# The softplus of a Mamba block summed by TensorE in an open PSUM bank

## The reference

```python
dt = jax.nn.softplus(dt_low @ W_dt + b_dt)      # 512 tokens x 512 channels
h = exp(dt_t[..., None] * A) * h + (dt_t * x_t)[..., None] * B_t[:, None, :]
y = einsum('bds,bs->bd', h, C_t)
y = (y + x * D) * silu(z);  return y @ W_out
```

## Time and profile before

| | |
|---|---|
| three executions | 4346.42, 4347.93, 4351.42 us, median 4347.93 |
| the profiled execution | 4355.29 us, its span 4353.5 us |
| busy share of TensorE, VectorE, ScalarE, GpSimd | 90%, 89%, 54%, 40% |
| granted TensorE clock, mean | 0.968 of 2.4 GHz |

### The profile page before, as it was taken

One profiled execution on the slowest core, in us unless ns is written; L12 is line 12 of the kernel. 1 busy time (PEld: TensorE's weight loads), 2 busy tenths in 40 slices (PEclk: granted clock), 3 DMA queues, 4 the chain that ended last, 5 costly groups with the idle time before them and its releaser, 6 DMA issues.

```text
span 4353.5 us, 55576 instructions
## 1 busy us (share of the span) xinstructions
PE 3935.7 (90%) x18933; PEld 2043.7 (47%) x18933; DVE 3872.0 (89%) x5708; ACT 2366.9 (54%) x4341; POOL 1724.7 (40%) x1295
## 2 busy tenths in 40 slices
PE   5878889999999999999999999998989999998898
PEld 3333444444545445454544545454444545544555
DVE  7699989898998989899898989989899899998753
ACT  2444455656555565555556465565545656564544
POOL 1254434443434435353343444444344344433410
PEclk9989999999999999899999999999899999999999
DMA  2699787878778787876787777788786888878511
GB/s 64 160 209 219 173 210 167 203 161 191 181 166 202 177 202 166 185 192 160 184 188 188 178 178 189 164 209 174 167 199 140 207 171 218 177 183 190 135 55 42
DMA packets 241440, 753.50 MB, mean 173 GB/s; under 512 B 37650, under 2 KB 132659, under 8 KB 171524
## 3 DMA queue, kind: packets, MB, share of 16 engines
q1 hardware_dynamic: 241156, 749.95, 73.7%
HBM read 647.30 MB, written 101.71 MB: 172 GB/s over the span
## 4 chain that ended last, share of the span: by engine, by line
DVE 40%; PE 33%; DMA 10%; issue 9%; ACT 6%; POOL 1%; SPq 1%; DVEq 0%; ACTq 0%; POOLq 0%
DVE state L1767 11%; DVE mt L1846 6%; DVE u L1762 4%; PE m L1249 4%; DMA state<-dtx_scratch 3%; PE m L1276 3%; PE pd L1477 2%; DMA decay<-dt_scratch 2%; PE y L1350 2%; DMA gz_scratch<-front 2%; DVE front L1701 2%; PE y L1338 2%; DVE front L1672 2%; DVE front L1676 2%; DVE front L1578 1%
## 5 line engine op out<-in xcount | busy, mean ns | idle before, releaser
L824 POOL TENSOR_TENSOR state<-state,bc 128x1024 f32<-128x1024 f32 x512 | 1270.4, 2482 | 1305.8 <-DVE u L1762 1287.1
L1767 DVE TENSOR_TENSOR_SCAN state<-decay,u 128x1024 f32<-128x1024 f32 x512 | 1166.8, 2279 | 6.4 <-ACT decay L1050 1.7
L1050 ACT ACTIVATE decay<-decay,a_neg 128x511 f32<-128x511 f32 x1024 | 674.9, 713 | 168.3 <-DMA decay<-dt_scratch 167.6
L1249 PE MATMUL m<-w_gu,hats_m 128*128 128x480 f32 x1472 | 680.5, 582 | 67.1 <-DVE front L1676 44.5
L1762 DVE TENSOR_TENSOR u<-state,bc 128x1024 f32<-128x1024 f32 x512 | 640.8, 1252 | 45.1 <-DMA state<-dtx_scratch 36.4
L1249 PEld LDWEIGHTS m<-w_gu,hats_m 128*128 128x128 f32 x1472 | 255.4, 192 | 334.5 <-issue 154.6
L805 POOL TENSOR_TENSOR front<-front,hsc_m 128x704 f32<-128x704 f32 x128 | 199.3, 1557 | 509.3 <-DVE front L1581 509.3
L1276 PE MATMUL m<-w_dn,front 128*128 128x256 f32 x1476 | 366.4, 390 | 14.1 <-ACT front L983 13.2
L1196 PE MATMUL y<-minus,zero 128*128 128x512 bf16 x1292 | 341.8, 389 | 2.1 <-ACT vec L904 2.1
L1338 PE MATMUL y<-state,sel 128*32 128x512 f32 x2048 | 280.6, 621 | 47.6 <-POOL state L824 47.3
L1276 PEld LDWEIGHTS m<-w_dn,front 128*128 128x128 f32 x1476 | 270.1, 191 | 103.8 <-ACT front L983 48.8
(11 more groups left out here) (396 smaller groups left out, 7278.3 us busy)
## 6 DMA issues: line engine op xcount, KB each, us to landing
decay<-dt_scratch SPq DMA_DIRECT2D x256, 1024.0 KB, 7.4
state<-dtx_scratch SPq DMA_DIRECT2D x256, 1024.0 KB, 11.5
qk_scratch_main<-shared SPq DMA_DIRECT2D x60, 384.0 KB, 4.3
shared<-qk_scratch_main SPq DMA_DIRECT2D x360, 64.0 KB
kh<-qk_scratch_main SPq DMA_DIRECT2D x360, 64.0 KB
xs_scratch<-front SPq DMA_DIRECT2D x16, 1024.0 KB, 9.5
dt_scratch<-front SPq DMA_DIRECT2D x256, 64.0 KB, 2.7
dtx_scratch<-hats_m SPq DMA_DIRECT2D x256, 64.0 KB, 5.0
```

The costliest lines, as they stand in the source:

```text
L824: eng.tensor_tensor(st, st, bc[:, 1:2, :].to_broadcast([P, WIDE, L]), ALU.mult).then_inc(scan_pool.sem, scan_pool.step(f"c{r}{h}"))
L1050: ins = eng.activation(d, d, ACT.Exp, scale=a_neg[:, g:g + 1])
L1249: mm = eng.matmul(f.bank(r, f"gu{t}{p}")[:, 0:2 * width], norm.hat_t[:, k, t * P:(t + 1) * P], w_gu[:, k, 2 * lo:2 * (lo + width)], start= ...
L1767: eng.tensor_tensor_scan(st, decay[:, n % ND, h * WIDE * L:(h + 1) * WIDE * L], u[:, :], 0.0, ALU.mult, ALU.add).then_inc(scan_dve.sem, sc ...
```

## The change

The logits are halved: `w_dt`, with the bias in its last row, is multiplied by 0.5 once at the start. Since max(a, 0) = a/2 + |a/2|, the whole softplus becomes a sum of six terms in the open bank: a/2, |a/2|, -(1 + ex) rounded, 1, ex and ln(1 + ex). TensorE adds each of the last five as an fp32 product with the identity (the constant 1 as a product of one row of ones with one row of ones). VectorE loses `rest`, `log` and `dt`, and reads the bank for `dtx`. ScalarE copies the sum out into `dt`, tokens 1 to 511. Two banks are used as before, in pairs of chunks.

```diff
 PE, head:
+    for first in (0, 2):
+        pair = (first, first + 1)
+        for c in pair:
+            # waits: c >= 2: ACT "dt{c - 2}"
+            matmul(MB[(1+c)%2], w_dt[:, c*P:(c+1)*P], pj, start=True, stop=False)    # dt{c}
+        for c in pair:
+            # waits: ACT "abs{c}"
+            matmul(MB[(1+c)%2], ident, lnx[:, c%2, :])                               # half{c}
+        for c in pair:
+            # waits: ACT "one{c}"
+            matmul(MB[(1+c)%2], ident, dt[:, c%2, :])
+            matmul(MB[(1+c)%2], ones[0:1].to_broadcast([1, P]), ones[0:1].to_broadcast([1, L]))
+            matmul(MB[(1+c)%2], ident, ex[:, c%2, :])                                # rest{c}
+        for c in pair:
+            # waits: ACT "ln{c}"
+            matmul(MB[(1+c)%2], ident, lnx[:, c%2, :], stop=True)                    # log{c}
-    matmul(MB[(1 + c) % 2], w_dt[...], pj, start=True, stop=True)   # waits: DVE "dt{c-2}"
 ACT:
+    mul(w_dt[:, :], w_dt[:, :], 0.5)                                # once, at the start
 ACT, head:
-    activation(ex, MB, Abs);  activation(ex, ex, Exp, scale=-1.0);  activation(dt, ex, Identity, bias=ones)
+    activation(lnx, MB, Abs); activation(ex, lnx, Exp, scale=-2.0)
+    activation(dt, ex, Identity, bias=less_one, scale=-1.0)
     activation(lnx[:, b, :], ex[:, b, :], Ln, bias=1.0)             # now after PE "half"
+    activation(dt[:, b, 1:L], MB[(c + b) % 2][:, 1:L], Copy)        # waits: DVE "dtx"
 DVE, head:
-    scalar_tensor_tensor(dt, dt, -1.0, ex, add, subtract)           # rest
-    tensor_tensor(lnx, lnx, dt, subtract)                           # log
-    scalar_tensor_tensor(dt, MB, 0.0, lnx, max, add)                # dt
-    tensor_tensor(dtx, dt, xs, mult)
+    tensor_tensor(dtx, MB[(1 + c) % 2], xs[:, c, :], mult)          # waits: PE "log{c}"
     memset(dt[:, b, 0:1], 0.0)
```

More of the change, by code:

```diff
@@ L96 @@
[L96 to L98 removed]
+        "11110000000000000000101201110001122111112222222222222222212122222222222211112221112222222222222122122112222222222222211222222111"
@@ L297, in build @@
         eps = sb("eps", [P, T])
-        ones = sb("ones", [P, 1])
+        ones, less_one = sb("ones", [P, 1]), sb("less_one", [P, 1])
         xx = sb("xx", [P, NX, T, D])
@@ L500, in build @@
         CONVS = [("conv", 0)] + [e for m in range(1, C) for e in (("conv", m), ("tanh", m - 1))] + [("tanh", C - 1)]
-        head_pe = Steps(sem("head_pe"), ["x0", "x1"] + [f"in{m}" for m in range(C)] + ["pj"] + [f"dt{c}" for c in range(C)]
+        head_pe = Steps(sem("head_pe"), ["x0", "x1"] + [f"in{m}" for m in range(C)] + ["pj"] + [f"{n}{c}" for b in (0, 2) for n in ("dt", "half", "rest", "log") for c in (b, b + 1)]
                         + [f"in{C + m}" for m in range(C)])
         head_act = Steps(sem("head_act"), ["x0", "x1"] + [f"{n}{m}" for n, m in CONVS] + ["pj"]
-                         + [f"{n}{c}" for b in (0, 2) for part in (("abs", "exp", "one"), ("ln",)) for c in (b, b + 1) for n in part] + [f"tanhz{m}" for m in range(C)])
+                         + [f"{n}{c}" for b in (0, 2) for part in (("abs", "exp", "one"), ("ln",), ("dt",)) for c in (b, b + 1) for n in part] + [f"tanhz{m}" for m in range(C)])
         head_dve = Steps(sem("head_dve"), [n for w, m in CONVS for n in ((f"tap{m}1", f"tap{m}2", f"tap{m}3") if w == "conv" else (f"silu{m}",))]
-                         + [f"{n}{c}" for c in range(C) for n in ("rest", "log", "dt", "dtx", "zero")] + [f"siluz{m}" for m in range(C)])
+                         + [f"{n}{c}" for c in range(C) for n in ("dtx", "zero")] + [f"siluz{m}" for m in range(C)])
         scan_pe = Steps(sem("scan_pe"), [n for r in range(ROUNDS) for n in ([f"skip{r // Q}"] if r % Q == 0 else []) + [f"sum{r}"]] + [f"o{t}" for t in range(T)])
@@ L772, in _ @@
             eng.memset(ones[:, :], 1.0)
+            eng.memset(less_one[:, :], -1.0)
             eng.memset(w_dn[:, IK - 1, :], 0.0)
@@ L1023, in head @@
                         eng.wait_ge(dt_saved[c % 2], 64 * (2 * i + 1))
-                    eng.activation(dt[:, c % 2, :], ex[:, c % 2, :], ACT.Identity, bias=ones[:, :]).then_inc(head_act.sem, head_act.step(f"one{c}"))
+                    eng.activation(dt[:, c % 2, :], ex[:, c % 2, :], ACT.Identity, bias=less_one[:, :], scale=-1.0
+                                   ).then_inc(head_act.sem, head_act.step(f"one{c}"))
                     if c % 2:
-                        yield
-                        if c >= 2:
-                            eng.wait_ge(head_dve.sem, head_dve.after(i, f"dt{c - 2}"))
                         for b in range(2):
+                            yield
+                            eng.wait_ge(head_pe.sem, head_pe.after(i, f"half{c - 1 + b}"))
                             eng.activation(lnx[:, b, :], ex[:, b, :], ACT.Ln, bias=1.0
                                            ).then_inc(head_act.sem, head_act.step(f"ln{c - 1 + b}"))
+                        for b in range(2):
+                            yield
+                            eng.wait_ge(head_dve.sem, head_dve.after(i, f"dtx{c - 1 + b}"))
+                            eng.activation(dt[:, b, 1:L], MB[(c + b) % 2][:, 1:L], ACT.Copy).then_inc(head_act.sem, head_act.step(f"dt{c - 1 + b}"))
                 for m in range(C):
```

352 lines of the change are left out of this document (181 added, 171 removed).

## The result

The changed kernel takes 4543.46 us, median of three executions (4536.49 to 4562.05), against 4347.93. The ratio is 1.0463, with a 95% interval of 1.0432 to 1.0495. The profiled execution took 4543.46 us, its span is 4541.7 us, which is 188 us more than before, and the granted clock has a mean of 0.982 (0.968 before).

What follows compares the result with a forecast made beforehand. TensorE's queue, late in the dt stretch, was taken to bound the kernel there: +215 for products, +13 for new waits, -56 for the clock make +172 us on 4355.3, less 7 to the median: 4520 us, range 4410 to 4630.

Steps and rivals of the forecast that it cites:

- products, seq. 3 to 15: Dt stretches of thirteen sequences: added fp32 products lengthen TensorE's work by 18.8 us a sequence, 244 us.
- keepers: TensorE's filler products in the dt stretches of sequences 3 to 15: nearly all of 19.5 us go, 16 us taken off.
- idle time filled: TensorE's idle 23.4 us in the dt stretches of sequences 3 to 15 is filled by added products, 23 us off.
- clock: Dt stretches: most drops to a lower TensorE clock go, giving back 56 us; bounds -110 and +66.
- sequences 0 to 2: Pipeline fill: 56 us added against 54 us of slack, mostly in the first two; 10 us for the third.
- new waits: dt2 waits for log0, dtx on VectorE and ScalarE's copy: 1 us a sequence, +13; bounds 0 and 3 us each.
- The queue that is late: Dt stretch, sequences 3 to 15: TensorE does real work in 383.1 of 426.0 us; its queue is late, +215 us together.
- The price of a product: TensorE: 0.88 us per identity product, 0.19 + 0.11 for the step to one row and back; 4.70 us a chunk.
- VectorE at nothing: VectorE loses 141 us of work, in its free quarter of the dt stretch: nothing more taken off; bounds 0 and -28.
- the first: Rival: the clock does not come back because new products wait for ScalarE one by one; +294, 4640 us; chance 0.18.
- The second's catch-up: Rival: clock gives back 110 us and VectorE's relief 20 to 30; +90, about 4440 us; chance 0.13.
- The third, VectorE as the bound: Rival: delayed queue catches up outside the dt stretch, relief and clock remain; -84 us, 4264 at best; chance 0.05.

Runs made afterwards that it cites:

- the run without them: Changed kernel with full products and order, but dtx, ScalarE's copy, next logits and z freed from the chain of new waits: 4531.89 us, ratio 1.0427.
- the run that filled it: Kernel before with nine more keepers ahead of dt2 in each of the seven sequences with clock drops: 4338.87 us, ratio 0.9988.
- The run with load put back: Changed kernel with three unused 128x512 VectorE operations after each dtx, the exponential of chunk c + 2 waiting for them: 4605.30 us, ratio 1.0600.
- the one with four products: Changed kernel with the constant 1 added by a second ScalarE activation instead of the product of ones: 4511.41 us, ratio 1.0380.

## Why the prediction was right

The forecast was 4520 us with a range of 4410 to 4630, slower by 172 us in the profiled execution; measured were 188 us between the spans and 195.5 between the medians. Term by term, forecast and measured (the row of the new waits is not added to the others, which hold it already):

| term | forecast | measured | from |
|---|---|---|---|
| products, seq. 3 to 15 | +244 | +250 | 52 x 4.81 us |
| keepers | -16 | -18.7 | 19.51 to 0.82 |
| idle time filled | -23 | -18.9 | 23.43 to 4.51 |
| work moved in by the order | 0 | +29, and -29 in the rest | 2294.8 to 2266.2 |
| clock | -56 | -49 to -62 (repeat: -33 to -51) | below |
| sequences 0 to 2 | +10 | +22 | 84.61 to 106.63 |
| new waits | +13 | 1 to 11 | idle for the copy; the run without them |
| rest, without the moved work | 0 | +12 | keepers +7, idle +5 |

- **The queue that is late.** Right. The argument was that real work filled 90% of the stretch on TensorE, so that every added product lengthens it. The stretch is 99.3% full after, grew by 13.8 us a sequence (forecast 12 to 15), and the kernel before with nothing but five products added costs 221 us. The period from dt0 to dt0 has a mean of 268 us over sequences 3 to 14, as forecast.
- **The price of a product.** 4.81 against 4.70 us a chunk. The step to one row and back costs about what the neighbour in the earlier trace rows said: 1.05 and 1.06 us for the ones, 0.96 to 1.05 for ex, against 1.07 and 0.99.
- **The clock.** Right in the change. TensorE's work without keepers grew by 216.5 us (383.1 to 599.6), and 250 + 29 - 216.5 leaves 62 for the clock; the windows' half-clock time fell from 116 to 18 us, which would be 49. Of the 13 us between, some 4 may be clock that the 29 hold (the half-clock time of the rest fell from 58 to 51 us); the others are not explained. In the second execution of the change the same two sums give 51 and 33 us. But -56 rests on a stretch that TensorE's queue fills: in the kernel before, refilling the gap freed 31 us of TensorE work and moved the time by 7. That the drops follow the gap behind the table load, as the prediction said, is supported by the run that filled it: five of seven went.
- The Trainium skill ("Perfetto Trace Analysis", section "Matmul Optimizations") says that the matmul engine scales its power with utilization, so that matmuls should be issued back to back. The five products on 128 rows agree (clock 1.00). The change agrees in the main (0.96 to 1.00; in its second execution 0.82 in a stretch with no idle time at all). The products on 17 rows do not agree: back to back, with TensorE busy 98.7% of the stretch, they had 0.58 to 0.74.
- **What was missed.** The sum left out that the new order moves other work into the stretch, 29 us. It costs nothing where it is moved out again, so the error cancelled, which was luck. Sequences 0 and 1 were taken as slack and cost 4 and 5 us, sequence 2 cost 13. The new waits were put too high and the rest of the sequences (+12) at nothing, and these two nearly cancel as well. The mechanism was right; that the number came so close owes something to chance.
- **A reading that was wrong.** The waits of the earlier trace rows, 17.7 and 10.7 us, add up the waits in front of the products and those in front of the weight loads ahead of them, which run side by side. The products alone stood idle for 4.2 and 3.2 us behind line 1721. So the 28 us that the prediction took as the most that VectorE's relief could give was some four times too much, and -28 was no bound that could have been reached in this way. It changed nothing, as the prediction took 0.
- **VectorE at nothing.** Its groups lose 137 us (forecast 141); the page, which counts overlapping instructions once, shows 118, hence 3754 and not 3730. The bounds were 0 and -28. The run with load put back says that VectorE's time counts on the new chain (62 us for three operations a chunk), more than "nothing" suggests. It does not measure the relief itself. The nearest comparison is the kernel before with five products, whose span is 22 us longer than that of the change. Most of it lies in sequences 0 to 2 (18 us) and in the rest (21 us, with 29 us of work moved out); the other way, the stretches of the change are 10.5 us longer, and what lies before, between and behind them 6 us. TensorE's idle time in the stretches is 18.4 us with five products in the kernel before and 4.5 in the change. Of the 18.4 us it had waited 6.5 for VectorE and nearly all others for ScalarE. What VectorE's relief gave is not shown by this.
- **The rivals.** The clock came back, so the first falls. The second's catch-up did not come: the rest of the sequences is 17 us shorter only because 29 us of work left it. The third, VectorE as the bound, needed the queue to catch up 172 us outside the stretches, and nothing was caught up there: without the moved work the rest is 12 us longer. VectorE is busy 94% of that rest in the change (96% before) and TensorE 93%, so the two stay close there.

What the prediction did not see is how close the next bounds stand. Remove the length, and TensorE stands idle for 85 to 108 us of the stretches, 35 to 42 of them for the copy and 14 to 17 for GpSimd's state; take the copy's waits away as well, and the time is still 1.0359 times that of before. The new order's moved work, the missing keepers, the other waits and the lower clock are all in that rest; they were not separated. A version of the new order with the old keepers and the products left out was not tried, so how much of the 188 us the order alone would cost stays open. No version of the change came below the kernel before; the best that computes it in full is the one with four products, 3.8% slower.

## What to carry to other kernels

Before moving work to another engine, read the stretch where it will stand and not the page: subtract the fillers, and if real work already fills 90% of it, the added work can cost nearly its full length, as it did here, whatever it saves elsewhere. Three vector operations of 0.7 us traded for five fp32 products of 0.86 to 1.06 us were then a loss. And when an experiment that takes the length away doesn't give the time back, look at what filled its place (the clock of each window, the next wait) before dropping the theory: add the length alone to the old kernel instead. And when a view gives the waits of a line, see whether they are those of the products or of the weight loads too: added up they overstate TensorE's idle time.

## What the runs showed of the hardware

- Five added fp32 products of 512 columns per chunk cost 221 us in the whole kernel when they read 128 rows (granted clock 1.00 in all thirteen stretches, mean 598 ns a record), and 552 us when they read 17 rows (0.58 to 0.74, mean 848 ns), with the same count and hardly a gap between them. The two runs differ in the number of rows and in the values of the operands, and these were not separated. Runs with products of one column had 0.61 to 0.90 as well, and those with bf16 products 0.69 to 0.99, both with idle time on TensorE. Whether rows, columns or gaps decide there was not separated.
- The clock of one stretch differs between executions of one kernel: 0.96 and 0.82 in sequence 7 of the change, with no idle time on TensorE in either.
- A product of one row of ones is not cheaper than a full one: 1.05 and 1.06 us from start to start with the step, against 0.85 to 0.96 for identity products.
- The multiplication by x, 128x512 in fp32, takes VectorE 688 ns with one operand in the PSUM bank (line 1747 of the change) and 794 ns with both in SBUF (line 1727 of the kernel before); with x times x from SBUF, in the change without the waits, it takes 820 ns. The prediction took 0.69 us for the bank, which holds, and called it the same as from SBUF, which does not. Why it differs was not tested.
